# The label row in the first bank, its masks directly behind the score masks

## The chip, the cores and the metric

The kernel runs on one core of one Trainium2 chip. The metric is the device time of one execution in microseconds (us), the median of three runs. TensorE (PE) multiplies into PSUM, which has eight banks of 512 f32 columns; VectorE (DVE), ScalarE (ACT) and GpSimd (POOL) do the element-wise work, and GpSimd works on SBUF alone here. SyncE (SP) issues most of the transfers. Each engine runs its own list of instructions in order; the kernel orders engines against each other by semaphores that it writes out by hand.

## The reference, cut to what matters

Two sandwiched blocks over x of 2 x 4096 tokens with 512 channels: `x = x + ln(attention(ln(x)))`, then `x = x + ln(ffn(ln(x)))`. The attention is linear (16 heads, ReLU on q and k). The second block is gated linear attention in chunks of 64 tokens over 8 heads of 64, once dense and once sparse, with four experts that share v:

```python
e = softmax(x @ We);  _, idx = top_k(e, 1);  mask = one_hot(idx, 4)
rw = e * mask
q_e, k_e, gk_e = q2 * rw, k2 * rw, gk2 * mask        # for each expert
o = gla(q1, k1, v, gk1) + sum over experts of gla(q_e, k_e, v, gk_e)
o = o * rsqrt(mean(o * o) + eps) * norm_w;  o = o * silu(g);  out = o @ Wo
```

Each token belongs to the one expert with the largest logit. Two tokens of a chunk act on each other in the sparse part only if they have the same expert and the later one comes second. The kernel builds that as a mask of 128 x 128: the expert's label of the column's token, compared with the label of the row's token, times a causal constant.

## The kernel before, in words

The first pass goes over all 64 tiles of 128 tokens in groups of four and sums the moments that the linear attention needs. The second pass, which the change is in, has one `step` for each of the 64 tiles, two to a loop iteration, with the function `step` of each engine giving the order of its work. A step works on three tiles at once: the front of tile n (projections, router, gates, decays, scores), the back of tile m = n - 1 (masks on its scores, its outputs, its gated norm), the output product of tile n - 2, and the attention part of tile n + 2.

Around the change one step goes like this.

VectorE (`step`, lines 1342 to 1381): it adds the state products of tile m to the carried state (`back_carry1`, `back_carry`, which reads banks 0 and 3), takes the maximum of the router's logits and the label `lab` of tile n, masks tile m's dense scores (`back_masks`, line 1172, banks 2 and 5, signals `am1_ok`) and its sparse scores with the mask `same_c` of tile m (`back_masks2`, line 1180, banks 4 and 6, signals `am2_ok`). Then, for tile n: `front_low` (lines 1227 to 1230, the low half of the low-rank activations, signals `low_ok`), `front_onehot` (line 1248 writes the one-hot `m4`, line 1251 its product `hm`), and `front_masks` (line 1263 writes `same_d`, a mask with the cumulation's constant, line 1264 writes `same_c`, signals `same_ok`). Then `back_select` (lines 1211 and 1214) picks each token's expert from the sparse product of tile m and signals `sel_ok`; then `back_join`, and for tile n `front_kmax`, `front_kdiff` (line 1292), `front_logsig` (line 1270, signals `ls_ok`) and further on `front_lslow` (line 1281, signals `lsl_ok`).

TensorE: `project_v` (bank 1), `label_bc` (line 362, a product of ones with the diagonal of the labels `lab_i` that ScalarE writes, which puts all labels in a row, here into bank 6), `inter_sparse` of tile m (line 483, banks 2 and 3 in its first half and 0 and 1 in its second), `gates` (lines 366 to 368, banks 4 to 6), `inter_dense` and `intra` (bank 7), `project_k2` (lines 367 and 368, bank 3, waits for `sel_ok`), `project_k`, `den` for tile n + 2 (bank 0), the output product, `cumulate` (lines 418 and 419, waits for `lsl_ok`, multiplies with `same_d`), and further projections, transposes and scores.

ScalarE takes the gates through Abs, Exp and Ln (`front_gates`, lines 745, 739, 741), which `front_logsig` needs. GpSimd adds the two masked score arrays (`back_am`, line 1038, when `am2_ok` comes), multiplies v with the one-hot (`front_vm`, line 1045) and does the decays and the gated norm.

A wait for `cur(n)` is for the signal of tile n, one for `prev(n)` for that of tile n - 1. The label row in bank 6 has to wait until the score masks have read bank 6 (`am2_ok`), and the gates, which overwrite bank 6, until both masks have read the row (`same_ok`):

```python
def gates(n):
    pe.wait_ge(S("low_ok"), cur(n))
    pe.wait_ge(S("am1_ok"), prev(n))
    pe.wait_ge(S("same_ok"), cur(n))
```

Of the kernel before, what the change touches and what calls it, by code (L numbers as in the profile page):

```python
# [5 lines left out]
P = 128  # L6
# [40 lines left out]
def sandwich_kernel(nc, x_d, wqkv_d, wproj_d, bproj_d, wb_d, wl_d, ws_d, wo_d, nw_d, consts_d, out_d):  # L47
# [11 lines left out]
    with ExitStack() as ctx:  # L59
        def sb(name, *shape, dt=f32):  # L60
            return ctx.enter_context(nc.sbuf_tensor(name, [P, *shape], dt))
# [98 lines left out]
        ones16 = sb("ones16", P, dt=f16)  # L160
        centred16, halves16 = sb("centred16", P, dt=f16), sb("halves16", 2, dt=f16)
        lab_i = sb("lab_i", P, dt=f16)
# [14 lines left out]
        bank = [psum[:, i, :] for i in range(8)]  # L177
# [4 lines left out]
        def S(name):  # L182
            if name not in sems:
                sems[name] = ctx.enter_context(nc.semaphore(name))
            return sems[name]
# [20 lines left out]
        def cur(n):  # L206
            return n + 2

        def prev(n):
            return n + 1  # L210
# [100 lines left out]
        def _(pe):  # L311
            mm = nc.tensor.matmul
# [45 lines left out]

            def label_bc(n):
                pe.wait_ge(S("labi_ok"), cur(n))  # L360
                pe.wait_ge(S("am2_ok"), prev(n))
                mm(bank[6][:, 0:P], ones16[:, :], lab_i[:, :], start=True, stop=True).then_inc(S("rx_pe"), 1)

            def second(out, which, k):
                if which == 1:
                    return mm(out, low[:, 1, :], ws[:, 0, k, :], start=True, stop=True)
                mm(out, low[:, which, :], ws[:, 0, k, :], start=True, stop=False)  # L367
                return mm(out, low[:, which, :], ws[:, 1, k, :], start=False, stop=True)  # L368

            def gates(n):  # L370
                pe.wait_ge(S("low_ok"), cur(n))
                pe.wait_ge(S("am1_ok"), prev(n))
                pe.wait_ge(S("same_ok"), cur(n))
                for k, which in ((0, 1), (1, 1), (2, 0)):
                    last = second(bank[4 + k], which, k)
                last.then_inc(S("g_pe"), 1)
# [6 lines left out]
            def project_v(n):  # L383
                pe.wait_ge(S("carry1_ok"), prev(n))
                wide(n, 1, 2 * C, "v_pe")
# [7 lines left out]
            def project_k(n, back):  # L393
                pe.wait_ge(S("ldiff_ok"), cur(n))
                if back:
                    pe.wait_ge(S("sel_ok"), (n - 1) * 4 + 4)
                for g in range(KT):
                    mm3(bank[2], lambda x: xnT[:, x, g, :], lambda x: wb[:, x, g, C:2 * C], g == 0, g == KT - 1)
# [5 lines left out]
            def project_q1(n):  # L404
                pe.wait_ge(S("ls_ok"), cur(n))
                wide(n, 5, 0, "q1_pe")
# [63 lines left out]
            def inter_sparse(n, front):  # L470
                pe.wait_ge(S("state_ok"), cur(n))
                pe.wait_ge(S("q2T_ok"), cur(n))
                pe.wait_ge(S("am1_ok"), cur(n))
                pe.wait_ge(S("carry_ok"), cur(n))
                if front:
                    pe.wait_ge(S("ldiff_ok"), cur(n + 1))
                for half in (1, 0):
                    if half == 0 and front:
                        pe.wait_ge(S("v_ok"), cur(n + 1))
                    for r in range(2):  # L480
                        for odd in range(2):
                            h = slice(odd * D2, odd * D2 + D2)
                            last = mm(psum[:, 2 * half + odd, r * 256:r * 256 + 256], q2T[h, 2 * half + r, :],  # L483
                                      statex[h, 2 * half + r, :], start=True, stop=True)
                last.then_inc(S("ix_pe"), 1)
# [31 lines left out]
            def step(n, p, b, front=True, back=True, tail=True, ahead=True, more=True, first=False):  # L517
                m, mp, t = n - 1, 1 - p, n - 2
                if front:
                    project_v(n)  # L520
                    label_bc(n)
                if back:
                    inter_sparse(m, front)
                if front:
                    if first:
                        pe.wait_ge(S("x1_ok"), cur(1))
                    gates(n)
                if back:
                    inter_dense(m, front)
                    intra(m, mp)  # L530
                if front:
                    project_k2(n, back)
                    project_k(n, back)
                if ahead:
                    den(n + 2, p, b, back=back)
                if tail:
                    out_mm(t, back)
                if front:
                    cumulate(n, back)
                    project_q1(n)  # L540
                    project_q2(n)
                    half_sums(n)
                if ahead:
                    y_mm(n + 2, b)
                if front:
                    transposes(n)
                    state_products(n, p, ahead)
                if front and more:
                    route(n + 1, tail, back)
                    low_rank(n + 1)  # L550
                if front:
                    scores(n, 0)
                    scores(n, 1)
# [568 lines left out]
        def _(dve):  # L1122
# [98 lines left out]
            def front_low(n):  # L1221
                dve.wait_ge(S("low1_ok"), cur(n))
                up, down = slice(0, LORA), slice(LORA, P)
                g, g_low, g_copy = slice(ROW_G, ROW_ONE), slice(0, 2 * GLR), slice(2 * GLR, 4 * GLR)
                parts = bank[7][:, 0:2 * P].rearrange("p (x c) -> p x c", x=2)
                minus = (ALU.mult, ALU.subtract)
                ve.scalar_tensor_tensor(low[down, 0:4:2, :], parts[up], LOW_SCALE, low[up, 0:4:2, :], *minus)
                ve.scalar_tensor_tensor(low[g_low, 1, :], parts[g, 0, :], LOW_SCALE, low[g, 1, :], *minus)
                ve.tensor_scalar(low[g_copy, 1, :], parts[g, 0, :], LOW_SCALE, None, ALU.mult)
                ve.scalar_tensor_tensor(low[up, 3, :], parts[down, 1, :], LOW_SCALE, low[down, 3, :], *minus).then_inc(S("low_ok"), 1)  # L1230
# [28 lines left out]
            def front_masks(n):  # L1259
                dve.wait_ge(S("rx_pe"), cur(n))  # L1260
                dve.wait_ge(S("cum_pe"), prev(n))
                row = bank[6][:, 0:P]
                ve.scalar_tensor_tensor(same_d[:, :], row, lab[:, :], centred, ALU.is_equal, ALU.mult)
                ve.scalar_tensor_tensor(same_c[:, :], row, lab[:, :], causal, ALU.is_equal, ALU.mult).then_inc(S("same_ok"), 1)

            def front_logsig(n):
# [75 lines left out]
            def step(n, p, b, front=True, back=True, tail=True, ahead=True, reset=False):  # L1342
                m, mp, t = n - 1, 1 - p, n - 2
                if back:
                    back_carry1(m, reset)
                    back_carry(m, reset)
                if front:
                    front_router(n)
                    front_label(n)
                if back:  # L1350
                    back_masks(m)
                    back_masks2(m)
                if front:
                    front_low(n)
                    front_onehot(n, p)
                    front_masks(n)
                if back:
                    back_select(m, mp)
                if front:
                    front_prob(n)  # L1360
                if back:
                    back_join(m)
                if front:
                    front_kmax(n)
                    front_kdiff(n)
                    front_logsig(n)
                if back:
                    back_norm(m)
                if front:
                    front_kfac(n)  # L1370
                    front_lslow(n)
                    front_sil(n, p, tail)
                if ahead:
                    ahead_qz(n + 2, p, b)
                    ahead_qz_split(n + 2)
                if front:
                    front_gated_1(n)
                    front_gated_q2(n)
                if tail:
                    back_out(t, p)  # L1380
                if front:
                    front_decay(n, p)
                if ahead:
                    ahead_residual(n + 2, p)
                    ahead_low(n + 2, p)
# [177 lines left out]
```

## Time and profile before

| | |
|---|---|
| median of 3 runs | 2603.74 us (2602.77 to 2603.75) |
| the profiled execution | 2605.18 us, span 2603.4 us |
| busy in the span | TensorE 93%, VectorE 70%, ScalarE 60%, GpSimd 46% |
| mean granted TensorE clock | 0.992 of full speed |
| chain that ended last | TensorE 61%, VectorE 17%, issue 10%, ScalarE 8% |

The span is the time from the first to the last instruction of one profiled execution. Matmuls are pipelined and the profile models their ends, so that a matmul's duration reaches past the start of the next, and a busy TensorE is not one at its peak. The chain is followed back from the last instruction to what released it at each step; "issue" is time in which an engine waited for nothing that the profile shows. A wait is put down to the signal that came last by the profile.

### The profile page before, as it was taken

How to read it: one execution, taken by the hardware profiler on the slowest of the kernel's cores; microseconds unless marked ns; L12 is line 12 of the kernel's file. 1: busy time of each engine (PE TensorE's matmuls, PEld its weight loads, DVE VectorE, ACT ScalarE, POOL GpSimd, SP SyncE). 2: the span in 40 equal slices, each digit the busy share in tenths (PEclk: the TensorE clock that was granted, in tenths of full speed). 3: DMA queues.
4: the chain of work that ended last, by engine and by line, in shares of the span. 5: the costliest groups of instructions: out<-in, count | busy, mean ns of one | idle time of the engine just before them, and what ended most of it. 6: DMA issues, size and time to landing. Idle time of an engine off the chain costs nothing.

```text
span 2603.4 us, 56298 instructions
## 1 busy us (share of the span) xinstructions
PE 2417.6 (93%) x20208; PEld 1439.4 (55%) x20208; DVE 1825.9 (70%) x3484; ACT 1554.6 (60%) x3281; POOL 1194.0 (46%) x929
## 2 busy tenths in 40 slices
PE   4999999988999999999999999999999999999997
PEld 2444444455555556565556555555666565655554
DVE  4444544337777777777777777777777777777775
ACT  3222322245676767766666767666776666776663
POOL 2796323323444444444444444444444444444444
PEclk9999999988999999999999999999999999999998
DMA  6434433211111111111111111111111111111111
GB/s 214 109 105 129 104 99 99 66 53 29 42 40 40 40 44 44 44 45 40 44 40 40 40 41 41 41 40 44 44 48 41 40 44 40 40 40 40 40 25 33
DMA packets 250704, 145.65 MB, mean 56 GB/s; under 512 B 208096, under 2 KB 208096, under 8 KB 250144
## 3 DMA queue, kind: packets, MB, share of 16 engines
q1 hardware_dynamic: 240048, 119.32, 18.4%
q10 hardware_dynamic: 9504, 17.31, 1.8%
q0 software_dynamic: 1104, 8.40, 0.9%
q8 instruction: 28, 0.46, 0.1%
q14 instruction: 20, 0.16, 0.0%
HBM read 61.09 MB, written 33.55 MB: 36 GB/s over the span
## 4 chain that ended last, share of the span: by engine, by line
PE 61%; DVE 17%; issue 10%; ACT 8%; POOL 2%; DMA 1%; SPq 1%; DVEq 0%; ACTq 0%; POOLq 0%
PE psum L319 12%; PE psum L321 12%; PE psum L320 12%; PE psum L580 6%; DVE region L1180 3%; DVE m L1248 3%; PE psum L492 2%; ACT junk L672 2%; DVE region L1201 2%; PE psum L503 2%; PE psum L331 2%; PE psum L437 2%; DVE region L1172 2%; PE psum L367 2%; ACT region L704 2%
## 5 line engine op out<-in xcount | busy, mean ns | idle before, releaser
L1050 POOL TENSOR_TENSOR region<-region,kfac 128x512 f32<-128x512 f32 x64 | 124.4, 1944 | 452.3 <-DVE kfac L1300 452.3
L319 PE MATMUL psum<-wb,region 128*128 128x512 f16 x768 | 294.3, 383 | 0.0
L320 PE MATMUL psum<-wb,region 128*128 128x512 f16 x768 | 293.3, 382 | 0.0
L321 PE MATMUL psum<-wb,region 128*128 128x512 f16 x768 | 293.2, 382 | 0.0
L1033 POOL TENSOR_TENSOR region<-region 128x1024 f32<-128x1024 f32 x64 | 147.8, 2309 | 266.1 <-DVE region L1404 234.0
L1404 DVE SCALAR_TENSOR_TENSOR region<-psum,region 128x512 f16<-128x512 f32 x64 | 44.3, 692 | 225.3 <-ACT region L862 225.3
L1038 POOL TENSOR_TENSOR region<-region 128x1024 f32<-128x1024 f32 x64 | 150.7, 2355 | 105.3 <-DVE region L1180 105.3
L1045 POOL TENSOR_SCALAR region<-region,m 128x512 f32<-128x512 f32 x256 | 172.2, 692 | 25.3 <-DVE hm L1251 24.5
L580 PE MATMUL psum<-region 128*128 128x512 f16 x768 | 176.3, 379 | 2.1 <-DVE region L1404 2.1
L745 ACT ACTIVATE region<-psum 128x1536 f32<-128x1536 f32 x64 | 92.9, 1451 | 124.9 <-PE psum L368 124.9
L1078 POOL TENSOR_TENSOR og<-og 128x512 f16<-128x512 f32 x64 | 74.2, 1160 | 191.8 <-ACT og L804 191.8
L1214 DVE SCALAR_TENSOR_TENSOR region<-psum,m,region 128x512 f32<-128x512 f32 x192 | 144.3, 751 | 6.8
L1166 DVE SCALAR_TENSOR_TENSOR region<-region,rstd 128x512 f16<-128x512 f32 x64 | 48.1, 752 | 143.1 <-ACT region L704 143.1
L1162 DVE SCALAR_TENSOR_TENSOR region<-psum,rstd,region 128x512 f32<-128x512 f32 x64 | 48.1, 751 | 140.9 <-issue 138.1
L1054 POOL TENSOR_TENSOR region<-region 128x512 f32<-128x512 f32 x64 | 81.2, 1269 | 141.9 <-ACT region L771 141.9
L680 ACT ACTIVATE region<-psum 128x512 f32<-128x512 f32 x256 | 137.3, 589 | 0.0
L1061 POOL TENSOR_TENSOR region<-region,decay 128x512 f32<-128x512 f32 x64 | 67.0, 1047 | 152.1 <-DVE decay L1317 152.1
L1400 DVE TENSOR_TENSOR region<-region 128x512 f16<-128x512 f32 x64 | 102.4, 1600 | 49.0 <-ACT region L875 49.0
L1270 DVE SCALAR_TENSOR_TENSOR region<-psum,region 128x1536 f32<-128x1536 f32 x64 | 112.5, 1758 | 32.2 <-ACT region L741 32.2
L447 PE MATMUL psum<-region 64*128 64x128 f32 x2048 | 131.6, 279 | 0.0
L483 PE MATMUL psum<-region 64*128 64x256 f32 x1024 | 127.9, 388 | 2.9 <-DVE region L1172 2.0
L757 ACT ACTIVATE region<-psum 128x512 f32<-128x512 f32 x64 | 38.2, 597 | 153.3 <-PE psum L321 153.3
(232 smaller groups left out, 7263.6 us busy)
## 6 DMA issues: line engine op xcount, KB each, us to landing
region<-x_in SPq DMA_DIRECT2D x128, 256.0 KB, 2.6
q_cols<-region ACTq DMA_DIRECT2D x64, 256.0 KB, 2.5
region<-q_cols SPq DMA_DIRECT2D x64, 256.0 KB, 2.8
out_rows<-region SPq DMA_DIRECT2D x62, 256.0 KB, 2.0
region<-wb_in POOLq DMA_DIRECT2D x1, 3072.0 KB, 11.7
region<-wqkv_in SPq DMA_DIRECT2D x4, 512.0 KB, 5.7
region<-region SPq DMA_TRANSPOSE x128, 3.0
region<-ws_in POOLq DMA_DIRECT2D x1, 1280.0 KB, 15.8
```

The lines of the kernel that those rows point to most:

```text
L319: mm(out, lhs(0), rhs(0), start=start, stop=False)
L320: mm(out, lhs(0), rhs(1), start=False, stop=False)
L321: return mm(out, lhs(1), rhs(0), start=False, stop=stop)
L447: last = mm(bank[where[odd]][:, pr * P:(pr + 1) * P], kT[h, pr, :], qT[h, pr, :], start=True, stop=True)
L483: last = mm(psum[:, 2 * half + odd, r * 256:r * 256 + 256], q2T[h, 2 * half + r, :], statex[h, 2 * half + r, :], start=True, stop=True)
L580: last = mm(bank[4 + j], xn8[:, p * GT + t, x * C + j * P:x * C + (j + 1) * P], k16[:, y_, :], start=first and begins, stop=final and ends ...
L680: ac(dst.rearrange("p a b -> p (a b)"), bank[where], ACT.Copy).then_inc(S(done), 1)
L1033: nc.gpsimd.tensor_tensor(kacc[b], kacc[b], k16, ALU.add).then_inc(S("kacc_ok"), 1)
L1038: nc.gpsimd.tensor_tensor(am1[:, :, :, :], am1[:, :, :, :], am2[:, :, :, :], ALU.add).then_inc(S("am_ok"), 1)
L1045: last = nc.gpsimd.tensor_scalar(vm[:, e, :], v[:, p, :], m4[:, p, e:e + 1], 1.0, ALU.mult, ALU.mult)
L1050: nc.gpsimd.tensor_tensor(kd.rearrange("p (h d) -> p h d", h=H2), kd.rearrange("p (h d) -> p h d", h=H2), kfac[:, :].unsqueeze(2).to_broad ...
L1214: ve.scalar_tensor_tensor(to, of[:, :, e, :], m4[:, p, e:e + 1], to, ALU.mult, ALU.add).then_inc(S("sel_ok"), 1)
```

## The change

The label row goes into bank 0 in place of bank 6. It waits for `carry_ok` of the tile before (bank 0 has been read) in place of `am2_ok`. The gates wait for `am2_ok` of the tile before in place of `same_ok`. The second half of the sparse product, which overwrites bank 0, waits for `same_ok`. VectorE takes the two masks directly behind `back_masks2`, ahead of `front_low` and `front_onehot`, with a wait for `am2_ok` ahead of the second, since it overwrites the `same_c` that `back_masks2` reads. In the first step, the wait for `x1_ok` moves ahead of the label row, and one for `same_ok` is put ahead of `den`.

```diff
             def label_bc(n):
                 pe.wait_ge(S("labi_ok"), cur(n))
-                pe.wait_ge(S("am2_ok"), prev(n))
-                mm(bank[6][:, 0:P], ones16[:, :], lab_i[:, :], start=True, stop=True).then_inc(S("rx_pe"), 1)
+                pe.wait_ge(S("carry_ok"), prev(n))
+                mm(bank[0][:, 0:P], ones16[:, :], lab_i[:, :], start=True, stop=True).then_inc(S("rx_pe"), 1)
...
             def gates(n):
                 pe.wait_ge(S("low_ok"), cur(n))
                 pe.wait_ge(S("am1_ok"), prev(n))
-                pe.wait_ge(S("same_ok"), cur(n))
+                pe.wait_ge(S("am2_ok"), prev(n))
...
                 for half in (1, 0):
                     if half == 0 and front:
                         pe.wait_ge(S("v_ok"), cur(n + 1))
+                        pe.wait_ge(S("same_ok"), cur(n + 1))
...
                 if front:
                     project_v(n)
-                    label_bc(n)
-                if back:
-                    inter_sparse(m, front)
-                if front:
                     if first:
                         pe.wait_ge(S("x1_ok"), cur(1))
+                    label_bc(n)
+                if back:
+                    inter_sparse(m, front)
+                if front:
                     gates(n)
...
                     project_k(n, back)
+                if first:
+                    pe.wait_ge(S("same_ok"), cur(n))
                 if ahead:
                     den(n + 2, p, b, back=back)
...
             def front_masks(n):
                 dve.wait_ge(S("rx_pe"), cur(n))
                 dve.wait_ge(S("cum_pe"), prev(n))
-                row = bank[6][:, 0:P]
+                row = bank[0][:, 0:P]
                 ve.scalar_tensor_tensor(same_d[:, :], row, lab[:, :], centred, ALU.is_equal, ALU.mult)
+                dve.wait_ge(S("am2_ok"), prev(n))
                 ve.scalar_tensor_tensor(same_c[:, :], row, lab[:, :], causal, ALU.is_equal, ALU.mult).then_inc(S("same_ok"), 1)
...
                     back_masks(m)
                     back_masks2(m)
                 if front:
+                    front_masks(n)
                     front_low(n)
                     front_onehot(n, p)
-                    front_masks(n)
                 if back:
                     back_select(m, mp)
```

## Rows read from the trace of the kernel before

**Rows 1.** View of waits: who waited for what; us in total, times, longest.
```profile
PE psum L366 <- DVE same_c L1264: 67.9, 64, 1.1
```

**Rows 2.** Chain of waits, one tile: start us, us, what.
```profile
1520.85 1.08 DVE m L1248
1522.51 0.27 DVE same_c L1264
```

**Rows 3.** Timeline of TensorE, the same tile: start us, us, instruction, idle before it.
```profile
1519.68 0.22 PE L362 MATMUL psum<-lab_i,ones 128*128 128x128 f16 x1
1519.84 2.00 PE L483 MATMUL psum<-region 64*128 64x256 f32 x16
1522.91 0.59 PE L366 MATMUL psum<-ws,region 128*128 128x512 f16 x2 [1.08 <-DVE same_c L1264]
1525.84 0.39 PE L367 MATMUL psum<-ws,region 128*128 128x512 f16 x1
1532.14 0.38 PE L321 MATMUL psum<-wo,ogT 128*128 128x512 f16 x1
1533.31 0.38 PE L418 MATMUL psum<-region,centred 128*128 128x512 f16 x1 [0.80 <-issue]
1536.55 0.38 PE L321 MATMUL psum<-wb,region 128*128 128x512 f16 x1
```

**Rows 4.** Timeline of VectorE, the same tile.
```profile
1516.78 0.21 DVE L1239 TENSOR_SCALAR ldiff<-psum,lmax 128x4 f32<-128x4 f32 x1
1518.18 1.28 DVE L1180 TENSOR_TENSOR region<-psum,same_c 128x512 f32<-128x512 f32 x2
1519.49 0.42 DVE L1227 SCALAR_TENSOR_TENSOR region<-psum,region 64x256 f16<-64x256 f32 x1
1520.52 0.29 DVE L1230 SCALAR_TENSOR_TENSOR region<-psum,region 64x128 f16<-64x128 f32 x1
1520.85 1.07 DVE L1248 TENSOR_SCALAR m<-cst,lab 128x4 f32<-128x4 f32 x1
1521.96 0.17 DVE L1251 TENSOR_TENSOR hm<-m,cst 128x8 f16<-128x8 f32 x1
1522.16 0.35 DVE L1263 SCALAR_TENSOR_TENSOR same_d<-psum,lab,cst 128x128 f16<-128x128 f32 x1
1522.42 0.34 DVE L1264 SCALAR_TENSOR_TENSOR same_c<-psum,lab,cst 128x128 f32<-128x128 f32 x1
1522.68 0.74 DVE L1211 TENSOR_SCALAR region<-psum,m 128x512 f32<-128x512 f32 x1
1527.29 0.69 DVE L1292 TENSOR_TENSOR region<-psum,kmax 128x512 f32<-128x512 f32 x1
1528.53 1.76 DVE L1270 SCALAR_TENSOR_TENSOR region<-psum,region 128x1536 f32<-128x1536 f32 x1 [0.55 <-ACT region L741]
1531.89 1.22 DVE L1281 SCALAR_TENSOR_TENSOR region<-region 128x1024 f16<-128x1024 f32 x1
1537.04 0.69 DVE L1305 SCALAR_TENSOR_TENSOR region<-psum,region 128x512 f32<-128x512 f32 x1 [1.11 <-PE psum L321]
```

**Rows 5.** Timeline of GpSimd, the first tile and the same tile.
```profile
573.10 4.58 POOL L1097 TENSOR_TENSOR mix<-wqk,mix 128x2048 f16<-128x2048 f32 x1 [0.15 <-POOL mix L1096]
...
1519.54 2.36 POOL L1038 TENSOR_TENSOR region<-region 128x1024 f32<-128x1024 f32 x1 [1.47 <-DVE region L1180]
1522.29 2.69 POOL L1045 TENSOR_SCALAR region<-region,m 128x512 f32<-128x512 f32 x4 [0.39 <-DVE hm L1251]
```

**Rows 6.** Timeline of the first tile, VectorE and TensorE.
```profile
576.80 0.90 DVE L1248 TENSOR_SCALAR m<-cst,lab 128x4 f32<-128x4 f32 x1
...
577.55 0.22 PE L362 MATMUL psum<-lab_i,ones 128*128 128x128 f16 x1
578.69 0.59 PE L366 MATMUL psum<-ws,region 128*128 128x512 f16 x2 [0.92 <-DVE same_c L1264]
```

**Rows 7.** The first mask's line: ns min/median/max, first and last start us.
```profile
L1263 DVE SCALAR_TENSOR_TENSOR same_d<-psum,lab,cst x64: 350/351/352, 577.9 to 2553.2; 128x128 f16<-128x128 f32 x64
```

More of the change, by code:

```diff
@@ L520, in step @@
                     project_v(n)
+                    if first:
+                        pe.wait_ge(S("x1_ok"), cur(1))
                     label_bc(n)
@@ L524, in step @@
                 if front:
-                    if first:
-                        pe.wait_ge(S("x1_ok"), cur(1))
                     gates(n)
@@ L533, in step @@
                     project_k(n, back)
+                if first:
+                    pe.wait_ge(S("same_ok"), cur(n))
                 if ahead:
```

## The prediction

> **What bounds the kernel now.** I read the view of waits first. It says who waits for the second mask: TensorE's gate matmuls (line 366) sit idle 67.9 us in 64 tiles, 1.06 us each, and the last thing that they wait for is the mask `same_c` (line 1264) [rows 1]. The chain of waits runs, in the tile that I take as the model, over the one-hot `m4` (line 1248, 1.08 us for four columns) and the second mask into the gates, so this idle time is on the path that sets the end and not beside it [rows 2]. Then TensorE's timeline of the same tile: from the label matmul on it stands still twice, 1.08 us before the gates and 0.80 us before the cumulation (line 418) [rows 3]. The second stall belongs to the first: gates feed Abs, Exp and Ln on ScalarE, these the log-sigmoid on VectorE (line 1270, for which VectorE sat idle 0.55 us), and its low half (line 1281) ends at 1531.89 + 1.22 = 1533.11, 0.20 before the cumulation starts [rows 3, 4]. So a gate that starts earlier pulls the cumulation forward, and everything behind it on TensorE up to the next tile's label matmul is work without a stall. What the change is worth is read between line 362 and line 418.
>
> **The change part by part**, in the model tile's times.
>
> *The label matmul* (line 362) runs 1519.68 to 1519.90, right behind the value projection, and stays there [rows 3]. Its new wait (`carry_ok`) is for additions that stand ahead of the score masks in VectorE's order, done before 1518.18 [rows 4]; it replaces a wait for `am2_ok`, which comes only at 1519.46. Cost nothing; if the carry were late the projection in front of it would be late as well.
>
> *The masks go ahead of four low-rank operations.* VectorE is through with the score masks (line 1180) at 1518.18 + 1.28 = 1519.46 and now has to wait for the row. From a matmul's end to a VectorE operation that waits for it the trace has 1536.55 + 0.38 = 1536.93 to 1537.04, so 0.11 [rows 3, 4]. The first mask starts at 1519.90 + 0.11 = 1520.01: a new wait of 0.55 us on VectorE, with the low-rank copies and all behind them queued there. The masks follow each other at 0.26 and the second takes 0.34 [rows 4]: it ends at 1520.61. The added wait between them is for line 1180, ended 0.8 earlier: nothing, unless the row came before 1519.46.
>
> *The low-rank operations* (lines 1227 to 1230) take 1519.49 to 1520.52 + 0.29 = 1520.81, so 1.32 [rows 4]. They could start as line 1211 does behind line 1264, 0.08 before the mask's end, or as line 1227 does behind line 1180, 0.03 after it [rows 4]. I take the second, it is the same instruction: 1520.64 to 1521.96. The Trainium skill, "VectorE: DVE Perf Modes", section "Two Vector instructions with no wait between them", says that an instruction whose operands begin in another group of 32 partitions than the last ones waits until all earlier ones are through; line 1227 writes to partitions 64 and up, and the trace's gap of 0.03 agrees. By that rule the gates gain 0.80 below, without it 0.91.
>
> *The gates* (line 366) started 0.15 after VectorE's release, 1522.42 + 0.34 = 1522.76 to 1522.91 [rows 3, 4]. They no longer wait for the masks but for `low_ok`, and start at 1521.96 + 0.15 = 1522.11: **0.80 us earlier**. The remaining two waits are for score masks done at 1519.46.
>
> *The sparse product's second half* gets the wait for both masks, since it overwrites bank 0. The product takes 1519.84 to 1521.84 [rows 3], its second half starts, as an estimate at half of that, near 1520.84; the masks release it at 1520.61 + 0.15 = 1520.76, and with the longest hop above (0.20) at 1520.81. Cost nothing, and behind it are 0.27 us of cover before the gates; beyond 0.35 us of lateness it costs the difference. Queued behind it are the gates, and back_select waits for it, which now starts at 1522.45.
>
> *The one-hot.* Line 1248 starts at 1520.85 and ends at 1521.92, just behind GpSimd's addition of the masked scores, 1519.54 + 2.36 = 1521.90. In the first tile, where another GpSimd operation runs, it ends at 576.80 + 0.90 = 577.70, and that operation at 573.10 + 4.58 = 577.68 [rows 4 to 6]. So most of its 1.07 is waiting for GpSimd. It now starts 1.15 later, at 1522.00, with that over. Bounds: 0.17 (line 1251) to 1.07; I take 0.21, the same operation on as many columns (line 1239) [rows 4]. It ends at 1522.21; the one-hot product 0.04 + 0.17 later, 1522.42; the selection (line 1211) 0.03 behind that, as line 1263 is behind line 1251 now, at 1522.45 against 1522.68: 0.23 earlier. The masks' 0.6 us have gone into a stall that was there.
>
> *What is late next.* From line 1211 to the end of line 1292 VectorE works through 1522.68 to 1527.98, 5.30 us [rows 4], so it is free for the log-sigmoid at 1527.75. ScalarE's logarithm moves with the gates by 0.80, and allows 1527.73. The log-sigmoid moves from 1528.53 to 1527.75, **0.78 us**, set by VectorE and ScalarE together. TensorE's `project_k2` (second line 367, 1525.84) waits for the selection and moves by 0.23 only, where the gates moved by 0.80: a new wait of some 0.57 us. It hides: TensorE would finish the output product at 1532.14 + 0.38 - 0.23 = 1532.29, and the cumulation can start at 1533.31 - 0.78 = 1532.53 [rows 3].
>
> *Sum.* Tiles 1 to 63: 63 x 0.78 = 49.1 us off. Tile 0 has no score masks and no addition on GpSimd; there the label row was done at 577.55 + 0.22 = 577.77 and the gates came 0.92 behind it, at 578.69 [rows 6], and now come 0.11 + 0.60 + 0.03 + 1.32 + 0.15 = 2.21 behind it: 1.3 us more. Its moved waits for `x1_ok` and `same_ok` are for work long done. Net 47.8 us. The profiled execution took 2605.18 (span 2603.40 and 1.78 around it): 2557.4. The median is 1.44 lower: 2603.74 - 47.8 = **2556 us**.
>
> **The rivals.**
> - *The one-hot costs 1.07 wherever it stands.* Then line 1211 starts at 1523.31, 0.63 later than now, the log-sigmoid at 1528.61, 0.08 later than now: 63 x 0.08 + 1.3 = 6.3, so 2610. For it: the length is nearly the same in all steady tiles. Against: it is 0.90 in tile 0, and ends with GpSimd both times.
> - *Slower: GpSimd holds up the masks.* They now lie wholly inside its addition. If they were blocked as line 1248 is, the first would start at 1521.92, the gates at 1521.92 + 0.60 + 0.03 + 1.32 + 0.15 = 1524.02, 1.11 later than now: 63 x 1.11 + 1.3 = 71, so 2675. It decides as soon as the first mask starts later than 1520.81. Against it: line 1263 took 350 to 352 ns in all 64 tiles [rows 7], and line 1264 ran under GpSimd's line 1045, which starts at 1522.29, at its 0.34 [rows 4, 5]. For it stands a rule of the Trainium skill, "SBUF — State Buffer", section "Who interferes with whom": a VectorE instruction with two inputs in SBUF is blocked by a GpSimd one that reads SBUF. The masks read a constant and the label column there; by the lengths just given the column doesn't count.
> - *Half the gain is used up on VectorE.* If the one-hot keeps some 0.44 us, or hops between the short operations eat 0.23, the selection isn't earlier at all; the log-sigmoid can then move only by the idle 0.55: 63 x 0.55 - 1.3 = 33, so 2570. The added waits and the queue behind them speak for it, nothing in a row does.
> - *More gain.* If the low-rank operations overlap the mask, the gates gain 0.91, the selection starts 0.34 earlier, and the log-sigmoid moves by 0.55 + 0.34, some 0.88: 2549.
>
> **How the numbers follow.** Forecast 0.70 (its own range 2550 to 2566: the hops and the one-hot's length, 0.1 us a tile being 6.3 us); half the gain 0.13; more 0.04; one-hot unshortened 0.08, of which 0.05 within 0.2% (5.2 us, what a measurement here can tell from no change) and 0.03 slower; masks blocked 0.05. Faster 0.70 + 0.13 + 0.04 = 0.87, same 0.05, slower 0.08. The range goes from the larger gain, with 3 us below it, over the half gain to 2585, where a third of the gain is left: 2546 to 2585. Outside lie the two cases without gain.
>
> **What would show it.** Right: the gates' idle time falls from 67.9 to under 25 us and ends with the low-rank operation of line 1230; line 1248 at about 0.2 us; a new wait of about 0.55 us on VectorE before the first mask, ended by the label matmul; one of about 0.5 us before project_k2; the one before the cumulation down to about 0.25. Wrong: line 1248 still near 1 us, the first mask starting with the end of GpSimd's addition, the sparse product longer than 2.2 us, or gates 0.8 us earlier and a cumulation that isn't.

## The result, and the profile after

| | before | changed |
|---|---|---|
| median, us | 2603.26 (2602.56 to 2603.75, 4 runs) | 2540.91 (2539.98 to 2542.99, 4 runs) |
| ratio, 95% interval | | 0.9762 (0.9745 to 0.9779) |
| the profiled execution: time, span, us | 2605.18, 2603.4 | 2541.0, 2539.2 |
| mean granted clock | 0.992 | 0.995 |

The kernel became 62.4 us faster. The prediction said 47.8 us, and 2540.91 lies below its range (2546 to 2585): the sign and the mechanism came as forecast, the size did not. One execution of all those below (of the masks between) took 2798.7 us at a granted clock of 0.849, where the others had 0.993 to 0.994, and is left out of its median.

The changed kernel's line numbers are higher by up to 4 (its gates are still line 366; the masks are 1266 and 1268, the one-hot 1251, the selection 1214, the log-sigmoid 1274). Engines' busy time and the chain that ended last, after:

```profile
PE 2412.6 (95%) x20208; PEld 1423.8 (56%) x20208; DVE 1770.0 (70%) x3484; ACT 1562.6 (62%) x3281; POOL 1194.1 (47%) x929
...
PE 79%; DVE 13%; issue 4%; POOL 3%; DMA 1%; ACT 1%; DVEq 0%; POOLq 0%; SPq 0%; ACTq 0%
```

TensorE's share of the chain was 61% before and is 79% now; ScalarE's 8% has become 1%. The groups of instructions by line, matmuls alone (busy us, mean ns of one | idle us before them, and what ended it), answer to [rows 1]:

```profile
L367 PE MATMUL psum<-ws,region 128*128 128x512 f16 x192 | 73.4, 382 | 39.0 <-DVE region L1217 39.0
L366 PE MATMUL psum<-ws,region 128*128 128x512 f16 x128 | 38.7, 384 | 10.1 <-DVE region L1233 2.1
```

The gates' 67.9 us of idle time are down to 10.1, and no mask ends them any more; where the profile names what ended them (2.1 us in the first tile), it is the last low-rank operation, line 1233. The new wait before `project_k2` is there, 39.0 us in all. Now one tile in the middle of a loop of the second pass, on TensorE, to be read against [rows 3] (start us, us, instruction, idle before it):

```profile
1396.71 0.22 PE L362 MATMUL psum<-lab_i,ones 128*128 128x128 f16 x1
1396.86 2.00 PE L484 MATMUL psum<-region 64*128 64x256 f32 x16
1398.98 0.60 PE L366 MATMUL psum<-ws,region 128*128 128x512 f16 x2
...
1402.59 0.39 PE L367 MATMUL psum<-ws,region 128*128 128x512 f16 x1 [0.61 <-DVE region L1217]
...
1409.44 0.38 PE L418 MATMUL psum<-region,centred 128*128 128x512 f16 x1 [0.17 <-issue]
...
1427.05 0.22 PE L362 MATMUL psum<-lab_i,ones 128*128 128x128 f16 x1
```

From the label matmul to the next one are 1427.05 - 1396.71 = 30.34 us. The gates start 2.27 us behind the label matmul, the cumulation 12.73. And VectorE in the same tile, to be read against [rows 4]:

```profile
1395.30 1.28 DVE L1183 TENSOR_TENSOR region<-psum,same_c 128x512 f32<-128x512 f32 x2
1396.96 0.35 DVE L1266 SCALAR_TENSOR_TENSOR same_d<-psum,lab,cst 128x128 f16<-128x128 f32 x1 [0.38 <-PE psum L362]
1397.23 0.34 DVE L1268 SCALAR_TENSOR_TENSOR same_c<-psum,lab,cst 128x128 f32<-128x128 f32 x1
1397.61 0.42 DVE L1230 SCALAR_TENSOR_TENSOR region<-psum,region 64x256 f16<-64x256 f32 x1
...
1398.63 0.29 DVE L1233 SCALAR_TENSOR_TENSOR region<-psum,region 64x128 f16<-64x128 f32 x1
1398.96 0.23 DVE L1251 TENSOR_SCALAR m<-cst,lab 128x4 f32<-128x4 f32 x1
1399.22 0.17 DVE L1254 TENSOR_TENSOR hm<-m,cst 128x8 f16<-128x8 f32 x1
1399.42 0.75 DVE L1214 TENSOR_SCALAR region<-psum,m 128x512 f32<-128x512 f32 x1
...
1404.06 0.69 DVE L1296 TENSOR_TENSOR region<-psum,kmax 128x512 f32<-128x512 f32 x1
1404.67 1.75 DVE L1274 SCALAR_TENSOR_TENSOR region<-psum,region 128x1536 f32<-128x1536 f32 x1
```

GpSimd's addition in the same tile, and below it the first mask and the one-hot over all tiles (ns min/median/max, first and last start), for [rows 5, 7]:

```profile
1396.66 2.36 POOL L1041 TENSOR_TENSOR region<-region 128x1024 f32<-128x1024 f32 x1 [1.56 <-DVE region L1183]
```
```profile
L1266 DVE SCALAR_TENSOR_TENSOR same_d<-psum,lab,cst x64: 350/351/353, 573.9 to 2487.0; 128x128 f16<-128x128 f32 x64
...
L1251 DVE TENSOR_SCALAR m<-cst,lab x64: 229/230/430, 575.9 to 2489.0; 128x4 f32<-128x4 f32 x64
```

The masks run at their old lengths though the addition (1396.66 to 1399.02) lies over them, and the one-hot takes 0.23 where it took 1.07 (230 ns in the median; the 430 is the first tile, where it again ended 0.03 behind a GpSimd operation). The log-sigmoid starts 7.96 us behind the label matmul and VectorE is not idle before it; over all tiles it waited for ScalarE once, before for 32.2 us in 64 tiles.

The first tile on TensorE, for [rows 6]:

```profile
573.66 0.22 PE L362 MATMUL psum<-lab_i,ones 128*128 128x128 f16 x1
575.93 0.61 PE L366 MATMUL psum<-ws,region 128*128 128x512 f16 x2 [2.06 <-DVE region L1233]
```

Here the gates come 2.05 behind the label row's end, 1.13 more than before.

For the comparison a tile of the same kind is needed. The model tile of the prediction, near 1520 us, turned out to be one of the few steps at the switch of the batch that the code writes out; 56 of the 64 tiles run in VectorE's loops. Two lines of VectorE of a loop tile before the change, and two of the model tile:

```profile
1422.90 0.15 DVE L1243 TENSOR_REDUCE lab<-lscore 128x1 f32<-128x4 f32 x1
1423.06 1.29 DVE L1172 TENSOR_TENSOR region<-psum,cst 128x512 f32<-128x512 f32 x2
...
1516.91 0.15 DVE L1243 TENSOR_REDUCE lab<-lscore 128x1 f32<-128x4 f32 x1
1516.97 1.29 DVE L1172 TENSOR_TENSOR region<-psum,cst 128x512 f32<-128x512 f32 x2
```

In the model tile line 1172 starts 0.06 behind the start of the label's reduction, in the loop tile 0.16: the loop has 0.1 us more there. TensorE in that loop tile before:

```profile
1425.69 0.22 PE L362 MATMUL psum<-lab_i,ones 128*128 128x128 f16 x1
...
1429.00 0.59 PE L366 MATMUL psum<-ws,region 128*128 128x512 f16 x2 [1.07 <-DVE same_c L1264]
...
1439.40 0.38 PE L418 MATMUL psum<-region,centred 128*128 128x512 f16 x1 [0.79 <-issue]
```

The next label matmul came at 1457.05, a period of 31.36. By these rows the gates came 3.31 behind the label matmul and the cumulation 13.71. So a tile in the loop gained 1.04 at the gates and 0.98 at the cumulation, and the rest of the period is nearly as it was (17.65 and 17.61 us). Over all tiles of the loops the label matmuls are 31.33 us apart before (median) and 30.34 after, so a tile gained 0.99. What goes beyond the 0.98 of the cumulation is the label matmul itself: before, it started 0.23 to 0.26 behind the matmul in front of it in the loops' tiles, late by its wait for the score masks; after, 0.21 to 0.22.

### The profile page after: what moved, and what is told of

Its sections match the earlier page's. It is cut to its first block, busy times and chain, and to the rows that moved or that the text cites. A ratio compares the mean times of both kernels' runs of the same rounds, so it can differ in the third digit from the quotient of the medians.

```text
span 2539.2 us, 56360 instructions
## 1 busy us (share of the span) xinstructions
PE 2412.6 (95%) x20208; PEld 1423.8 (56%) x20208; DVE 1770.0 (70%) x3484; ACT 1562.6 (62%) x3281; POOL 1194.1 (47%) x929
## 4 chain that ended last, share of the span: by engine, by line
PE 79%; DVE 13%; issue 4%; POOL 3%; DMA 1%; ACT 1%; DVEq 0%; POOLq 0%; SPq 0%; ACTq 0%
PE psum L319 17%; PE psum L320 16%; PE psum L321 16%; PE psum L583 6%; DVE region L1217 6%; PE psum L447 5%; PE psum L437 4%; PE psum L464 4%; PE psum L331 2%; DVE region L1214 2%; PE psum L456 2%; PE psum L418 2%; PE psum L367 1%; PE psum L419 1%; PE psum L368 1%
## 5 line engine op out<-in xcount | busy, mean ns | idle before, releaser
L319 PE MATMUL psum<-wqk,region 128*128 128x512 f16 x256 | 98.0, 383 | 34.3 <-DMA region<-region 34.3
```

The lines of the kernel that those rows point to most:

```text
L319: mm(out, lhs(0), rhs(0), start=start, stop=False)
```

## The experiments

Each kernel ran beside the kernel before (2601.87 to 2604.54 as its median in the various sets). The theory: all of the gain is that a one-hot which waits 0.85 us for GpSimd no longer stands between the label row and the gates. Rivals: the other bank and its freer waits do it; the one-hot can be cured in place; the written-out steps and the loop are the whole of the missed size.

**The order alone.** The kernel before with the masks moved up; the row stays in bank 6 with its old waits.

```diff
                 if front:
+                    front_masks(n)
                     front_low(n)
                     front_onehot(n, p)
-                    front_masks(n)
```

> The kernel before with one part of the change: VectorE takes the two masks directly behind the score masks; the label row stays in bank 6, waits for am2_ok, and the gates wait for same_ok. Theory (the one-hot's wait for GpSimd, which stood between the label row and the gates, is what the change took away; the bank does not matter): both masks are done 1.3 us before the low-rank operations are, so the gates start when they do after the whole change; 2541 us, up to 2547 if the row's wait for am2_ok makes it 0.1 us late in each tile. Rival (the bank counts: the row must come before the score masks are through, and the gates must be free of the masks): at least half the gain is lost, 2570 us or more.

Measured: 2543.14 us, ratio 0.9766 (0.9750 to 0.9783). The changed kernel's ratio is 0.9762, its interval nearly the same: in the times, the bank and the exchanged waits together contribute nothing that can be told apart from zero. The trace allows them a little: here the label matmuls of the loops' tiles are 30.36 us apart (median), against 30.34 in the changed kernel, which makes 1 to 2 us in all.

**The bank alone.** The changed kernel with `front_masks(n)` put back behind the one-hot.

```diff
                 if front:
-                    front_masks(n)
                     front_low(n)
                     front_onehot(n, p)
+                    front_masks(n)
```

> The other part alone: label row in bank 0, the gates free of same_ok, the second half of the sparse product waiting for it, the masks at their old place behind the one-hot. Theory: slower than before. same_ok comes 3.1 us after the label row, the second half then starts some 2 us later than it could, the gates behind it 0.8 us later than now, and the selection later as well: 63 x 0.8 = 50 us, 2654 us. Rival (the bank gives the gain): the gates no longer wait for the masks, 2604 us or less.

Measured: 2739.71 us, ratio 1.0526 (1.0509 to 1.0544). Slower, as expected, but by 135 us where about 50 were. TensorE in one tile:

```profile
1444.94 0.22 PE L362 MATMUL psum<-lab_i,ones 128*128 128x128 f16 x1
...
1448.28 1.86 PE L484 MATMUL psum<-region 64*128 64x256 f32 x8 [2.05 <-DVE same_c L1268]
1450.08 1.03 PE L366 MATMUL psum<-ws,region 128*128 128x512 f16 x2
```

The window over its second half (length; busy us of PE, PEld, DVE, ACT, POOL with their counts; granted clock; DMA), and of all tiles the gates' matmuls (ns min/median/max) and the wait (us in total, times, longest):

```profile
1448.00:1451.50 3.50, 3.22 (x12) 1.57 (x12) 1.31 (x3) 0.00 (x0) 2.34 (x4) 0.58 0.00 0
```
```profile
L366 PE MATMUL psum<-ws,region x128: 379/609/634, 574.7 to 2685.6; 128*128 128x512 f16 x128
```
```profile
PE psum L484 <- DVE same_c L1268: 127.4, 63, 2.1
```

The second half of the sparse product stands still for 2.05 us, and when it goes on the granted clock is 0.58 in that stretch, that is mostly at the lower of the two levels (1.2 GHz); the two gate matmuls of line 366 take 1.03 us against 0.60. It is so in most tiles: the wait comes in 63, and the median of these matmuls is 609 ns, 384 in the changed kernel. The mean clock of the run is 0.965. The wait was in the expectation, the clock after it was not, and the wait was also taken too short. The second half goes on 3.34 behind the label matmul; with the 1.00 that half of the product takes at full clock the gates would come 4.34 behind it, 1.03 later than before (3.31) and not 0.8. By this estimate the wait alone costs 63 x 1.03 = 65 us. The rest is of the size that the two mean clocks give, an estimate again: 2734 x (0.995 - 0.965) = 82 us of TensorE's time. Wait and clock were not tried apart.

**The one-hot ahead of the score masks**, the kernel before otherwise: if it is only the addition that holds it, it should be short there.

```diff
                     front_label(n)
+                    front_onehot(n, p)
                 if back:
                     back_masks(m)
...
                     front_low(n)
-                    front_onehot(n, p)
                     front_masks(n)
```

> The kernel before with one edit that the change does not have: the one-hot and its product are taken directly behind the label, ahead of the score masks, where GpSimd's addition has not begun. Order of masks and low-rank operations, bank and waits are those of before. Theory (what counts is that the one-hot's wait for GpSimd is off the way to the gates): line 1248 takes about 0.23 us, everything behind it on VectorE comes 0.4 us later up to the low-rank operations and 0.5 to 0.6 us earlier from the masks on; the row's wait for am2_ok makes TensorE 0.45 us late, gates some 0.7 to 0.8 us and log-sigmoid some 0.9 us earlier than before: 2545 to 2555 us. Rival (the place of the masks ahead of the low-rank operations counts): gain under 0.25 us a tile, 2590 us or more.

Measured: 2610.85 us, ratio 1.0027 (1.0017 to 1.0037). A miss: no gain, 0.3% slower. GpSimd, VectorE and TensorE in one tile:

```profile
1423.31 1.15 POOL L1078 TENSOR_TENSOR og<-og 128x512 f16<-128x512 f32 x1 [3.07 <-ACT og L804]
...
1423.48 1.01 DVE L1248 TENSOR_SCALAR m<-cst,lab 128x4 f32<-128x4 f32 x1
...
1427.33 0.22 PE L362 MATMUL psum<-lab_i,ones 128*128 128x128 f16 x1 [1.09 <-DVE region L1180]
```

There another GpSimd operation runs, which the expectation left out: it ends at 1424.46, the one-hot at 1424.49. The stall only moved, now ahead of the score masks; the label row, which in bank 6 needs them, comes 1.09 late. The one-hot again ends with a GpSimd operation, another one this time, which speaks for the cause; and "early" is no place for a cure.

**The masks between the low-rank operations and the one-hot**, the kernel before otherwise, row in bank 6.

```diff
                     front_low(n)
-                    front_onehot(n, p)
                     front_masks(n)
+                    front_onehot(n, p)
```

> The kernel before with the order low-rank operations, masks, one-hot; bank 6 and all waits as before. Theory: the low-rank operations fill the time in which VectorE waits for the label row after the change (0.4 us), the masks come right behind, and the gates are then held by TensorE's own work only, some 0.3 us earlier than after the change; the one-hot runs into GpSimd's addition again (about 0.5 us in place of 0.23) but ends with it, so that the selection comes 0.1 to 0.2 us earlier than after the change: 2533 us (2528 to 2538). Rival (the one-hot's wait costs as much here as it did ahead of the masks, or masks first is what counts): 2541 us or more.

Measured: 2534.54 us, ratio 0.9735 (0.9716 to 0.9755). TensorE, VectorE and GpSimd's addition in one tile:

```profile
1426.89 0.22 PE L362 MATMUL psum<-lab_i,ones 128*128 128x128 f16 x1
1427.12 2.00 PE L483 MATMUL psum<-region 64*128 64x256 f32 x16
1429.05 0.60 PE L366 MATMUL psum<-ws,region 128*128 128x512 f16 x2
```
```profile
1428.39 0.34 DVE L1264 SCALAR_TENSOR_TENSOR same_c<-psum,lab,cst 128x128 f32<-128x128 f32 x1
1428.65 0.55 DVE L1248 TENSOR_SCALAR m<-cst,lab 128x4 f32<-128x4 f32 x1
...
1429.35 0.75 DVE L1211 TENSOR_SCALAR region<-psum,m 128x512 f32<-128x512 f32 x1
```
```profile
1426.82 2.36 POOL L1038 TENSOR_TENSOR region<-region 128x1024 f32<-128x1024 f32 x1 [1.57 <-DVE region L1180]
```

The gates follow the sparse product without a gap, 2.16 behind the label matmul, and VectorE doesn't wait for the row, because the low-rank operations fill that time. The one-hot is at 0.55 and again ends (1429.20) with GpSimd's addition (1426.82 + 2.36 = 1429.18): it still waits, but where it costs less than the wait for the row did, for the selection starts 2.46 behind the label matmul against 2.71 in the changed kernel.

**The one-hot from PSUM**, at its old place: it compares the logits with their maximum in place of the score with the label, so that its wide input is not in SBUF.

```diff
-                ve.tensor_scalar(m4[:, p, :], score, lab[:, :], None, ALU.is_equal).then_inc(S("m4_ok"), 1)
+                ve.tensor_scalar(m4[:, p, :], bank[7][:, 2 * P:2 * P + NEXP], lmax[:, :], None, ALU.is_equal).then_inc(S("m4_ok"), 1)
```

> The kernel before with one operand changed: line 1248 makes the one-hot from the router's logits in PSUM (logit equal to the maximum) in place of the label and a constant in SBUF. Everything else, the order too, is as before. Theory (line 1248 is long only because it needs the SBUF port that GpSimd's addition holds): with its input in PSUM it takes about 0.2 us. What follows depends on the product behind it (line 1251), which has two inputs in SBUF: if that is blocked as well, it ends with GpSimd's addition (its 0.17 becomes about 1.0) and the time stays at 2604; if not, masks and gates come 0.85 us earlier: 2604 - 63 x 0.85 = 2550 us. The first is the likelier by the Trainium skill's page on the SBUF. Rival (line 1248 is slow by itself, or waits for something else): it keeps 1.07 us, 2604 us.

Measured: 2583.79 us, ratio 0.9931 (0.9915 to 0.9946), between the two outcomes. VectorE in one tile, and GpSimd's addition there:

```profile
1448.75 0.22 DVE L1248 TENSOR_SCALAR m<-psum,lmax 128x4 f32<-128x4 f32 x1
1449.01 0.82 DVE L1251 TENSOR_TENSOR hm<-m,cst 128x8 f16<-128x8 f32 x1
1449.75 0.34 DVE L1263 SCALAR_TENSOR_TENSOR same_d<-psum,lab,cst 128x128 f16<-128x128 f32 x1
```
```profile
1447.44 2.35 POOL L1038 TENSOR_TENSOR region<-region 128x1024 f32<-128x1024 f32 x1 [1.58 <-DVE region L1180]
```

The one-hot has its 0.22: with its wide input out of SBUF it no longer waits (its column of one element for each partition is in SBUF both times). But its product `hm`, eight columns and 0.17 us until now, takes 0.82 and ends (1449.83) with the addition (1449.79): it has two inputs in SBUF, and the stall passed to it. The Trainium skill, "SBUF — State Buffer", section "Who interferes with whom", says that a VectorE instruction with two inputs in SBUF contends with a GpSimd one that reads SBUF; the trace agrees for `hm` with this 0.82. The masks, whose second SBUF input is such a column, show no stall under the addition in the changed kernel, at 0.35 and 0.34. The one-hot of the kernel before had no more than a wide input and a column in SBUF either, and was stalled; what sets it apart from the masks, no run here shows. The gain is what used to come behind the addition's end: there the first mask started 0.26 behind it (1522.16 against 1521.90 [rows 4, 5]), here 0.04 ahead of it (1449.75 against 1449.79); 63 x 0.30 = 19 us, and 18 were measured.

**VectorE's loops written out**, in the kernel before and in the changed one, to measure what made the model tile differ.

```diff
-            with dve.Fori(2, TILES - 2, 2) as n:
+            for n in range(2, TILES - 2, 2):
...
-            with dve.Fori(TILES + 2, ALL - 2, 2) as n:
+            for n in range(TILES + 2, ALL - 2, 2):
```

> The kernel before with VectorE's two second-pass loops written out, step by step, same order and same waits. In the trace of before the tiles in the loops take 31.33 us and the four written-out steps at the batch switch 31.24, the first score mask starting 0.09 us later behind the label in the loops. Theory (the loop's register-valued waits cost VectorE that 0.09 us, on the path): the 56 tiles take 31.24 as well, 2604 - 5 = 2599 us. Rival (these tiles are shorter for another reason, their place at the batch switch): no change, 2604 us.

> The changed kernel with VectorE's two second-pass loops written out. Theory: after the change VectorE waits for the label row in every tile (0.36 us in the loop tiles, 0.48 in the written-out ones), so 0.09 us ahead of that wait gives nothing: 2541 us as the changed kernel. Rival (the 0.09 us is lost somewhere behind the row too): 2536 us or less.

Measured: before, written out, 2598.49 us, ratio 0.9983 (0.9974 to 0.9992); changed, written out, 2539.30, ratio to the kernel before 0.9755 (0.9742 to 0.9768), so no difference from 0.9762. VectorE of the kernel before, written out:

```profile
1420.45 0.15 DVE L1243 TENSOR_REDUCE lab<-lscore 128x1 f32<-128x4 f32 x1
1420.52 1.29 DVE L1172 TENSOR_TENSOR region<-psum,cst 128x512 f32<-128x512 f32 x2
```

The gap is the model tile's, and the period is now 31.25 nearly throughout, where the loops had 31.33. So some 0.08 us of the loop's 0.1 was on the path before. In the changed kernel it lies in front of VectorE's wait for the label row, which takes up most of it: the period is 30.34 with the loops and 30.32 written out. That is 0.06 us a tile of gain that the model tile could not show, 3 to 4 us in 56 tiles, and so not the whole of the 14.6 that the prediction missed.

**The one-hot between the two score masks**, the kernel before otherwise. Here GpSimd is idle: line 1078 is over and the addition has not begun.

```diff
                     back_masks(m)
+                if front:
+                    front_onehot(n, p)
+                if back:
                     back_masks2(m)
                 if front:
                     front_low(n)
-                    front_onehot(n, p)
                     front_masks(n)
```

> The kernel before with the one-hot and its product taken between the two score masks; ahead of them both, the one-hot had run into another GpSimd operation (line 1078) and kept 1.0 us. Between the masks GpSimd has nothing to do in the trace of before (from 1518.07 to 1519.54). Theory (the one-hot's place beside GpSimd's work is what counts, not the masks' place ahead of the low-rank operations, nor the bank): line 1248 takes 0.23 us; the second score mask, and with it the label row in bank 6, comes some 0.4 us later, the gates 0.7 us and the log-sigmoid 0.78 us earlier than before: 2555 us (2548 to 2562). Rival (the masks must come ahead of the low-rank operations): 2590 us or more.

Measured: 2560.16 us, ratio 0.9841 (0.9826 to 0.9856). VectorE's one-hot and TensorE's label row in one tile:

```profile
1434.87 0.22 DVE L1248 TENSOR_SCALAR m<-cst,lab 128x4 f32<-128x4 f32 x1
```
```profile
1436.73 0.22 PE L362 MATMUL psum<-lab_i,ones 128*128 128x128 f16 x1 [0.30 <-DVE region L1180]
```

With not one mask ahead of a low-rank operation, a one-hot that doesn't stall gives 42 of the 62 us on its own. What is missing to the changed kernel begins in the second line: the row in bank 6 now comes late, for the score masks are behind the one-hot. It starts 0.67 behind the matmul in front of it (median), where 0.22 is usual, and so 0.45 late (the 0.30 of idle time is less, since the profile lets a matmul reach past the start of the next). The log-sigmoid comes 7.80 behind the row against 7.96 in the changed kernel, which gives back 0.16. The label matmuls are 30.65 us apart against 30.34; 63 x 0.31 = 20.

**The changed kernel again, and the masks between again**, on one chip in five rounds, to settle which is faster.

> The changed kernel once more, beside the next one and the kernel before on one chip: 2541 us, 0.976 of before, if nothing depends on the chip.

> The order low-rank operations, masks, one-hot, with the label row left in bank 6, beside the changed kernel on one chip. Theory (its tiles take 30.22 us against 30.34): 63 x 0.12 = 7.5 us below the changed kernel, 2533 us. Rival (the two do not differ beyond what executions scatter): within 3 us of it.

Measured: the changed kernel 2541.55 us (2540.93 to 2541.82), ratio 0.9764 (0.9750 to 0.9777); the masks between 2535.21 (2533.73 to 2535.51), ratio 0.9737 (0.9723 to 0.9750). The two sets of times don't touch: low-rank, masks, one-hot, with the bank and the waits of before, is 6.3 us faster than the changed kernel, and beats both.

## Why the prediction was off, point by point

**The step that failed** is the first term of the sum, "63 x 0.78", which was sized too small. The mechanism in it is right; a tile gains 0.97 at the log-sigmoid (8.93 us behind the label matmul before, 7.96 after) and 0.98 at the cumulation. Three parts of the difference of 0.19:
- *The model tile*, 0.08. There the log-sigmoid came 1528.53 - 1519.68 = 8.85 behind the label matmul, in a loop tile 8.93. For 0.06 of it the kernel before with its loops written out shows that the loop is the reason (8.86 there, 8.92 in the loops, as medians).
- *The hops*, the times from the end of an instruction on one engine to the start of one on another engine that waits for it. From the label matmul's end to the first mask I took 0.11; it is 1396.96 - 1396.93 = 0.03. From the low-rank end to the gates I took 0.15; it is 1398.98 - 1398.92 = 0.06. Both figures were of other pairs of instructions. At the gates that makes 0.16 with the small differences of the lengths (forecast 2.43 behind the label matmul, measured 2.27); on VectorE's own path, by which the log-sigmoid is set, 0.06 (selection 2.77 and 2.71 behind it).
- *The log-sigmoid's start*, 0.05. I let it begin where line 1296 ends, with VectorE free; it begins 0.08 before that (1404.67 against 1404.75), as line 1211 does behind line 1264, a kind of start that the prediction names for the low-rank operations and does not take. The stretch from selection to line 1296 came out 0.03 longer.

Together 63 x 0.19 = 12 us. The first tile pays 1.13 (gates 2.05 behind the label row, before 0.92), where I had 1.3. By these terms the change is worth 63 x 0.97 - 1.13 = 60.0. From the first selection to the last one (lines 1211 and 1214) the profiles have 1968.1 and 1906.8 us, 61.3 apart. Of what the profiled pair differs by beyond that, 2.5 us lie ahead of tile 1's selection (611.5 and 609.0), and are not the change's: with the changed order it came at 610.2 in the repeat and at 612.1 in the written-out kernel. The granted clock there differs from execution to execution (0.68 in 570 to 580 us before, 1.00 after).

Two small terms stand in no sum. One is the label matmul, late by 0.02 to 0.04 us in the loops' tiles before and not after; the prediction put its wait at nothing, which is what the model tile has. The other is tile 1, which the prediction took to be like the rest. Its cumulation waits much longer, before, after, and in the repeat of the changed kernel:

```profile
622.08 0.59 PE L418 MATMUL psum<-region,centred 128*128 128x512 f16 x1 [3.30 <-issue]
```
```profile
618.98 0.58 PE L418 MATMUL psum<-region,centred 128*128 128x512 f16 x1 [2.67 <-issue]
```
```profile
620.25 0.38 PE L418 MATMUL psum<-region,centred 128*128 128x512 f16 x1 [2.67 <-issue]
```

Before, the granted clock from there to 625 us was 0.50, and tile 1's label matmul and the next one lie 33.81 us apart in place of 31.33. In the profile after, the clock was 0.72 to 625 us and the spacing 31.98; in the repeat it was 1.00, and 30.32. So tile 1 gains 1.8 to 3.5 us, where the sum has one of 0.97.

**What held.** *The one-hot*: 0.23 for a forecast 0.21 (229 to 230 ns except in the first tile). *The queue behind the masks*: the low-rank operations start 0.04 behind the second mask, forecast 0.03, and the rival with an overlap didn't come. *The new waits*: 0.38 for the row (forecast 0.55; the hop was shorter, and the loop's time takes some of it), 0.61 before project_k2 (0.57), 0.17 before the cumulation (0.25). *The sparse product* stays at 2.00 and its second half waits for nothing. *The hidden wait*: the 0.61 before project_k2 costs nothing, since the cumulation is still ended by the log-sigmoid's chain: it starts 4.77 behind the log-sigmoid, and 4.78 before. The chain that ended last runs over project_k2's wait in the profile after (line 1217 has 6% of it), because the view puts the 0.17 before the cumulation down to "issue" and stays on TensorE there.

**The rivals.** Half the gain, the one-hot unshortened and the masks blocked were wrong. So was the larger gain as I described it, though its 2549 was nearest: it came by other means than the one named. The range's lower end rested on it with 3 us to spare, and all hops were taken from the long side: errors of one sign in a term that is multiplied by 63.

**What I wouldn't have said before the runs**: the change has a part that is not needed. The new bank allows the row to be written early, but its old wait (`am2_ok`) held it up by only 0.02 to 0.04 us in nearly all tiles of the loops, and for the order as changed the old bank does as well within 1 to 2 us. Without the order the bank costs 135 us, since the masks then hold up the sparse product and a lower clock follows.

## What to carry to other kernels

A short operation that stalls on a shared resource is charged for the other's end, not for its own length: move it behind that end, or put work between that needs doing anyway, and look up what the other engine does at the new place first. Take the model tile from the loop, by the spacing of all tiles, and the price of a hop from the same pair of engines and kinds of instruction, since a tenth of a microsecond is multiplied by the number of tiles. When a change has two parts, the one that moves the order may be nearly all of it.

## What the runs showed of the hardware

- A one-hot of 128 x 4 elements ended 0.02 to 0.04 us behind three different GpSimd operations, whichever ran (lines 1038, 1078 and, in the first tile, 1097 [rows 4 to 6]), at lengths from 0.55 to 1.08 us in the tiles shown; alone it took 0.22 to 0.23.
- VectorE's loop cost some 0.1 us a tile in front of line 1172 (0.16 against 0.06 to 0.07 written out); by what instruction was not tried.
- With a wait of 2.05 us in each tile on TensorE (the bank alone), the granted clock was 0.58 from 1448.0 to 1451.5 us, as the work went on; the run took 135 us more, where the wait by itself, as estimated above, makes 65. Behind the 1.07 us that the gates waited in the kernel before, it stayed at 1.00 (1429 to 1432 us).
- The length of a wait did not settle the clock by itself. In tile 1 the cumulation waited 2.66 to 2.67 us in four profiles with the changed order (the changed kernel, its repeat, its loops written out, the order alone); from there to 625 us the granted clock was 0.72 in the first and 1.00 in the other three. Behind the 3.30 us of the kernel before it was 0.50.
